# A decoder block on one Trainium2 core: expert tiles ordered by token group, two accumulators, and the final normalisation moved into the tile loop

## The reference

```
shared = (silu(x @ shared_gate.T) * (x @ shared_up.T)) @ shared_down.T
probs = sigmoid(x @ router_w.T + routing_bias)
scores, indices = top_k(probs, 2);  scores = scores / sum(scores)
w[t, indices[t]] += scores[t]                      # 8 experts, 2 per token
combined = sum_e w[:, e] * ((silu(x @ gate_w[e]) * (x @ up_w[e])) @ down_w[e])
x = layernorm(x + shared + combined)               # no gain, eps 1e-5
```

## Time and profile before

| | us |
|---|---|
| median of 3 runs (lowest, highest) | 1850.27 (1849.88, 1854.23) |
| profiled execution: time / span in the trace | 1854.46 / 1852.8 |
| TensorE busy | 1686.3 (91% of the span) |
| VectorE, ScalarE, POOL busy | 1183.4, 807.0, 720.3 |
| tile loop: first y starts / last y starts | 1147.3 / 1800.36 |
| from the last y's end to the end of the span | 52.0 |

### The profile page before, as it was taken

The page is one execution under the profiler, slowest core; times in us unless marked ns, Lnnn a source line. Parts: engine busy times, 40 slices in busy tenths (PEclk is TensorE's granted clock), DMA queues, the critical chain, the costliest instruction groups (busy, mean ns, idle before and its releaser), DMA issues.

```text
span 1852.8 us, 35774 instructions
## 1 busy us (share of the span) xinstructions
PE 1686.3 (91%) x9652; PEld 1435.5 (77%) x9653; DVE 1183.4 (64%) x2682; ACT 807.0 (44%) x1507; POOL 720.3 (39%) x625
## 2 busy tenths in 40 slices
PE   6999968999947999999999997999999999999980
PEld 5777747888845888888888875888888888888870
DVE  6888867888835676676666766555555555555546
ACT  5888766777622323223233243333333333333326
POOL 1111117888822345445344354333333333333333
PEclk9999988999977999999999998999999999999995
DMA  4555475777633222222232244333333333333329
GB/s 140 180 197 201 154 260 149 248 248 248 230 114 129 70 94 81 81 104 78 72 104 81 80 161 133 53 58 53 58 53 58 53 56 55 56 55 53 58 44 362
DMA packets 137705, 220.64 MB, mean 119 GB/s; under 512 B 40544, under 2 KB 110368, under 8 KB 129328
## 3 DMA queue, kind: packets, MB, share of 16 engines
q1 hardware_dynamic: 112064, 184.44, 30.2%
q0 software_dynamic: 25584, 35.54, 10.9%
HBM read 122.79 MB, written 97.12 MB: 119 GB/s over the span
## 4 chain that ended last, share of the span: by engine, by line
PE 38%; DMA 16%; issue 6%; DVE 4%; POOL 3%; ACT 2%; SPq 0%; POOLq 0%; ACTq 0%; another core or an unknown queue 0%; DVEq 0%
DMA acc<-back_y,back_token 14%; PE back_ps L2482 10%; PE back_ps L2384 5%; PE back_ps L2502 5%; PE back_ps L2370 4%; PE back_ps L2361 3%; PE back_ps L2280 2%; POOL back_turned_qk L1733 2%; PE back_ps L2315 2%; ACT back_out L1901 2%; PE back_ps L2323 2%; PE back_ps L2491 1%; DVE back_y L2237 1%; PE back_ps L2302 1%; PE back_ps L2268 1%
## 5 line engine op out<-in xcount | busy, mean ns | idle before, releaser
L2482 PE MATMUL back_ps<-back_w_gu,back_xe_T 128*128 x1620 | 413.0, 404 | 1.5 <-DVE back_xe_T L2218 1.5
L1764 POOL DMA_INDIRECT acc<-back_y,back_token x135 | 209.2, 1549 | 461.5 <-DVE back_y L2237 364.2
L2482 PEld LDWEIGHTS back_ps<-back_w_gu,back_xe_T 128*128 128x128 f32 x1620 | 297.4, 189 | 61.6 <-issue 2.4
L2502 PE MATMUL back_ps<-back_w_down,back_he_T 128*128 x1620 | 225.3, 288 | 1.5 <-DVE back_he_T L2230 1.5
L2502 PEld LDWEIGHTS back_ps<-back_w_down,back_he_T 128*128 128x128 f32 x1620 | 200.7, 188 | 1.8 <-issue 1.7
L1183 PE MATMUL front_ps<-front_xn_T,front_w_in_parts 128*128 128x512 f32 x768 | 187.7, 401 | 5.2 <-issue 3.3
L1721 POOL DMA_INDIRECT sorted<-back_x,back_slot x128 | 136.7, 1068 | 135.1 <-DVE back_slot L2050 100.8
L1183 PEld LDWEIGHTS front_ps<-front_xn_T,front_w_in_parts 128*128 128x128 f32 x768 | 144.3, 191 | 42.1 <-issue 6.3
L2226 DVE TENSOR_TENSOR back_h<-back_h,back_ps 128x512 f32<-128x512 f32 x135 | 92.9, 688 | 121.3 <-PE back_ps L2482 121.3
L1014 DVE SCALAR_TENSOR_TENSOR front_conv<-front_ps,front_conv_wb,front_conv 128x508 f32<-128x508 f32 (+2 forms) x192 | 140.8, 740 | 43.7 <-ACT front_conv L844 38.0
L1895 ACT ACTIVATE back_he_T<-back_ps 128x512 fp32r<-128x512 f32 x135 | 80.8, 599 | 199.9 <-PE back_ps L2491 199.9
(11 more groups left out here) (230 smaller groups left out, 3010.8 us busy)
## 6 DMA issues: line engine op xcount, KB each, us to landing
back_xe<-sorted SPq DMA_DIRECT2D x135, 136.0 KB, 2.5
gate_T<-front_gate_T SPq DMA_DIRECT2D x16, 1024.0 KB, 4.7
xc_T<-front_xc_T SPq DMA_DIRECT2D x16, 1024.0 KB, 5.6
front_xc_in<-xc_T SPq DMA_DIRECT2D x16, 1024.0 KB, 5.3
front_gate_in<-gate_T SPq DMA_DIRECT2D x16, 1024.0 KB, 6.4
front_x_rows<-in_x SPq DMA_DIRECT2D x16, 512.0 KB, 5.4
front_c_rep<-c_parts SPq DMA_DIRECT2D x128, 64.0 KB, 4.2
front_rows_in<-in_x SPq DMA_DIRECT2D x16, 512.0 KB, 7.1
```

Of the source, the lines that this page charges most:

```text
L1764: pool.indirect_dma_start(out=d["acc"][:, :], out_offset=bass.IndirectOffsetOnAxis(ap=token[:, r:r + 1], axis=0), in_=y[:, r % 2], in_offs ...
L2482: op = nc.tensor.matmul(dst[:, r % 2], xe_T[:, x_part, k], w_gu[:, bass.ds(e, 1), m, w_part, k], start=(n == 0), stop=(n == len(PASSES) - 1))
L2502: op = nc.tensor.matmul(ps_y[:, 0:D_MODEL], he_T[:, h_part, k], w_down[:, bass.ds(e, 1), w_part, k], start=(n == 0), stop=(n == len(DOWN_P ...
```

## The change

Five things change together.

1. The tiles come in the order of token groups. `run` is kept for every group, `plan_tiles` counts for each group and expert how many tiles have been opened by then, and a slot's number is the running sum over (group, expert). So the first 8 (g + 1) + 7 tiles hold all rows of groups 0 to g.
2. Tiles with an even number add to `acc`, those with an odd one to a second DRAM tensor, `more`, which SP clears group by group during the first stage. An add waits for the add two before it. Rows that don't belong to a tile are sent to 128 spare rows (`spare`) and no longer to a real token with weight zero.
3. From quad 5 on, each turn of the loop also handles half a group of 256 tokens, five quads behind: SP loads the half from `acc` and `more` (512 KB), VectorE adds them (r = 1) and takes the moments (r = 2), POOL takes the root (r = 2), VectorE makes the bias and ScalarE normalises two slices (r = 3), SP stores 256 KB in the next quad. 29 of 32 halves are handled so, and three (`end_...`) after the loop.
4. Token numbers are kept in float32, and the order of tokens within a half is changed so that a half is one piece of memory.
5. The part of SBUF for POOL's DMA descriptors is halved (`dynamic_dma_scratch_size=8192`), and the buffers for the halves lie in what is gained.

```diff
+        def in_quads(eng, body):
+            body(0, False)
+            with eng.Fori(1, BEHIND) as quad:
+                body(quad, False)
+            body(BEHIND, False, 0)
+            with eng.Fori(BEHIND + 1, QUADS - 1) as quad:
+                body(quad, False, quad - BEHIND)
+            body(QUADS - 1, True, QUADS - 1 - BEHIND)
...
                     if not (last and r >= tiles - 2):
                         rows(i + 2, (r + 2) % 4)
+                    if f is not None:
+                        half(f, r, last)
                     if not (last and r == tiles - 1):
                         up(i + 1, (r + 1) % 4)
...
+                    sp.dma_start(d["more_rows"][a], pad[:, 0:D_MODEL].unsqueeze(1).to_broadcast([P, GS, D_MODEL])
+                                 ).then_inc(more_cleared, 16)
...
             def body(quad, last, f=None):
                 for r in range(LAST - 2 if last else 4):
                     sp.wait_ge(row_ready, 2 * (4 * quad + r + 1))
                     load(4 * quad + r + 2, r % 2, 4 * quad + r + 1)
+                    if f is not None and r == 0:
+                        if not is_at(f, 0):
+                            store_half(f - 1)
+                            sp.wait_ge(half_sum_ready, f)
+                        sp.wait_ge(added[0], 16 * (2 * f + 8))
+                        sp.wait_ge(added[1], 16 * (2 * f + 7))
+                        for dst, src in ((half_in, "acc_half"), (half_more, "more_half")):
+                            sp.dma_start(dst, d[src][f]).then_inc(half_loaded, 16)
-            sp.wait_ge(added, 16 * TILES)
-            for g in range(GROUPS):
-                sp.dma_start(total[:, g], d["acc_rows"][g]).then_inc(total_loaded[g], 16)
-            for g in range(GROUPS):
-                sp.wait_ge(out_ready, GS * (g + 1))
-                sp.dma_start(d["out"][g], out[:, g]).then_inc(out_stored, 16)
+            store_half(HALVES - 4)
+            sp.wait_ge(e_up_done, TILES)
+            sp.wait_ge(added[0], 16 * 4 * GROUPS)
+            sp.wait_ge(added[1], 16 * (4 * GROUPS - 1))
+            load_end(0)
+            sp.wait_ge(added[0], 16 * ((TILES + 1) // 2))
+            sp.wait_ge(added[1], 16 * (TILES // 2))
+            load_end(1)
+            load_end(2)
...
             def add(i, r):
                 pool.wait_ge(y_ready, i + 1)
-                if not is_at(i, 0):
-                    pool.wait_ge(added, 16 * i)
+                if not early(i):
+                    pool.wait_ge(added[r % 2], 8 * (i - r % 2))
                 pool.indirect_dma_start(
-                    out=d["acc"][:, :], out_offset=bass.IndirectOffsetOnAxis(
+                    out=d[("acc", "more")[r % 2]][:, :], out_offset=bass.IndirectOffsetOnAxis(
                         ap=token[:, r:r + 1], axis=0),
-                    in_=y[:, r % 2], in_offset=None, compute_op=ALU.add).then_inc(added, 16)
+                    in_=y[:, r % 2], in_offset=None, compute_op=ALU.add).then_inc(added[r % 2], 16)
...
+            def normalise_half(f):
+                act.wait_ge(half_bias_ready, f + 1)
+                for s in range(HALF):
+                    nc.scalar.activation(half_sum[:, s], half_sum[:, s], ACT.Identity, scale=half_rstd[:, s:s + 1],
+                                         bias=half_bias[:, s:s + 1]).then_inc(half_out_ready, 1)
...
+            def half(f, r, last):
+                if r == 1:
+                    add_half(f)
+                if r == 2:
+                    half_moments(f)
+                if r == 3:
+                    half_bias_of(f)
...
-    nc = bacc.Bacc("TRN2", target_bir_lowering=False, num_devices=1)
+    nc = bacc.Bacc("TRN2", target_bir_lowering=False, num_devices=1, dynamic_dma_scratch_size=8192)
```

More of the change, by code:

```diff
@@ L1406, in decoder_back @@
         slot_f = at("slot_f", small + 2.3125, [P, 2, GS])
[L1407 to L1411, removed]
+        run = at("run", -1.75, [P, GROUPS + 1, EXPERTS])
+        count_i = at("count_i", -7.75, [P, GROUPS + 1, EXPERTS], I32)
+        tiles = at("tiles", -7.125, [P, GROUPS + 1, EXPERTS])
+        opened = at("opened", -6.5, [P, GROUPS, EXPERTS])
+        before_tile = at("before_tile", -6, [P, GROUPS, EXPERTS])
+        ends = at("ends", -5.5, [P, 3, GROUPS * EXPERTS])
+        columns = at("columns", 194.59375, [P, 2 * GS + 3])
+        spare = at("spare", -1.1875, [P, SLOT_TILES])
         neg_half = at("neg_half", 194.65625, [P, 2 * GS])
@@ L1569, in early, with no_half, in_tiles @@
             return isinstance(g, int) and g < 2
+        def in_quads(eng, body):
[6 more added lines that the diff above has]
+            body(QUADS - 1, True, QUADS - 1 - BEHIND)
         def no_tile(i, r):
             pass
-        def in_tiles(eng, turn_x, up, turn_h, down, rows=no_tile):
+        def no_half(f, r, last):
+            pass
+        def in_tiles(eng, turn_x, up, turn_h, down, rows=no_tile, half=no_half, end_tile=2):
             rows(0, 0)
@@ L1580, in in_tiles, with body @@
             turn_x(1, 1)
-            def body(quad, last):
+            def body(quad, last, f=None):
                 tiles = LAST if last else 4
@@ L1697, in _, with store_half, body @@
             store_base(GROUPS - 1)
-            def body(quad, last):
+            def store_half(f):
+                sp.wait_ge(half_out_ready, HALF * (f + 1))
+                sp.dma_start(d["out_half"][f], half_sum).then_inc(half_stored, 16)
+            def body(quad, last, f=None):
                 for r in range(LAST - 2 if last else 4):
@@ L1782, in _ @@
+            for n in range(3):
+                end_root(n)
         @block.scalar
@@ L2074, in plan_tiles @@
                 dve.wait_ge(places, PLACES * GROUPS)
-                then(nc.vector.tensor_tensor(count_i, run, plan[:, PLAN_LESS], ALU.subtract))
+                last = EXPERTS - 1
+                less = plan[:, PLAN_LESS].unsqueeze(1)
+                at_ends = ends[:, 0].rearrange("p (g e) -> p g e", g=GROUPS)
+                end_steps = ends[:, 2].rearrange("p (g e) -> p g e", g=GROUPS)
+                rows_end = run[:, GROUPS:]
+                first_rows = before_tile.rearrange("p g e -> p (g e)")
@@ L2076, in plan_tiles @@
+                then(nc.vector.tensor_tensor(count_i, run, less.to_broadcast([P, GROUPS + 1, EXPERTS]), ALU.subtract))
                 then(nc.vector.tensor_scalar(count_i, count_i, 7, None, ALU.arith_shift_right))
                 then(nc.vector.tensor_copy(tiles, count_i))
-                then(nc.vector.tensor_tensor_scan(ends[:, 0], plan[:, PLAN_ONES], tiles, 0.0, ALU.mult, ALU.add))
-                then(nc.vector.tensor_scalar(ends[:, 1], tiles, -float(P), float(REGION), ALU.mult, ALU.add))
@@ L2080, in plan_tiles @@
-                then(nc.vector.tensor_tensor(ends[:, 2, 0:EXPERTS - 1], run[:, 1:], run[:, 0:EXPERTS - 1], ALU.subtract))
-                then(nc.vector.memset(ends[:, 2, EXPERTS - 1:], -1e6))
+                then(nc.vector.tensor_tensor(opened, tiles[:, 1:], tiles[:, 0:GROUPS], ALU.subtract))
+                then(nc.vector.tensor_tensor_scan(ends[:, 0], plan[:, PLAN_ONES], opened.rearrange("p g e -> p (g e)"), 0.0,
+                                                  ALU.mult, ALU.add))
+                then(nc.vector.tensor_tensor(before_tile, tiles[:, 1:], at_ends, ALU.subtract))
@@ L2259, in _ @@
+            in_tiles(dve, turn_x, up, turn_h, down, rows, half)
+            half_bias_of(HALVES - 4)
+            end_moments(0)
+            end_bias_of(0)
+            for n in (1, 2):
+                end_moments(n)
+            for n in (1, 2):
+                end_bias_of(n)
         @block.tensor
@@ L2450, in add_ends @@
                 pe.wait_ge(planned, PLANNED + COEF)
-                for q, of in enumerate((None, 1, 2)):
-                    lhs = plan[0:EXPERTS, PLAN_UNIT] if of is None else coef[:, of]
-                    op = nc.tensor.matmul(ps_plan[:, q], lhs, past, start=True, stop=True)
+                changes = slice(0, P - 1)
+                nc.tensor.matmul(ps_plan[0:1, 0], columns[changes, 2 * GS + 2:], past[changes], start=True, stop=True)
+                for q in (1, 2):
+                    op = nc.tensor.matmul(ps_plan[:, q], coef[changes, q], past[changes], start=True, stop=True)
                 op.then_inc(ends_turned, 1)
@@ L2554 @@
            "delta": [TOKENS], "x1": [GROUPS, P, GS, D_MODEL],
-           "sorted": [SORTED, ROW], "acc": [TOKENS + P, D_MODEL]}
+           "sorted": [SORTED, ROW], "acc": [TOKENS + P, D_MODEL],
+           "more": [TOKENS + P, D_MODEL]}
 def program(nc, t):
```

228 lines of the change are left out of this document (155 added, 73 removed).

## The result

| | before | after |
|---|---|---|
| median of 19 runs each (lowest, highest), us | 1852.67 (1849.65, 1854.23) | 1854.64 (1849.87, 1859.35) |
| profiled execution: time / span | 1854.46 / 1852.8 | 1853.05 / 1851.1 |

The ratio of after to before is 1.0014, 95% interval 1.0008 to 1.0021: 2.6 us slower, well inside the 0.3% that count as no change. The forecast was 15 us faster, with a range up to 1847; the time lies outside it.

What follows compares the result with a forecast made beforehand. TensorE was taken to pace the 135 tiles, with a 52.0 us tail where it does nothing. Terms -33.1 + 16.8 + 1.0 + 0.3 = -15.0 us took 1850.3 to 1835.3 us; range 1816 to 1847.

Steps and rivals of the forecast that it cites:

- What bounds the kernel: Tile loop: TensorE paces the 135 tiles, 4.885 us each; the add chain costs nothing until the end.
- The rival in which the adds set the pace: Tile loop: adds pace the tiles, so two accumulators quicken the loop by 13 us, to 1822; chance 3%.
- The tail, -33.1: After the last y: 52.0 us shrinks to 18.9 with only three halves left, saving 33.1 us.
- The loop, +16.8: Tile loop: normalisations ahead of the silu make TensorE start 0.6 us late at r = 3, 28 times.
- slack of 0.42 us: Tile loop: h could end 0.42 us later before delaying TensorE's transposes, so r = 2 loses nothing.
- 1.0 each (28 us) if the statistics at r = 2 overrun too: Tile loop: upper bound of the loss per half; as a rival, slips near 1 us each give 1846, chance 8%.
- The start, +1.3: Before the tiles: 1.0 us for the longer plan and 0.3 for clears and an extra register instruction a group.
- my 1.0 for what reaches the first y: Plan of the tiles: 2.1 us more VectorE work, of which 1.0 delays the first tile; bounds 0 and 2.1.
- the clears I took 0.3: Before the tiles: sixteen 512 KB clears of `more` in SP's queue, with register instructions, cost 0.3 us; bounds 0 and 3.
- the halved descriptor space I took 0: POOL's scatters: halving the descriptor store costs nothing; the other bound was 2 us or more for each of 128 scatters.
- transfers of the halves holding up tiles: Tile loop: loads in SP's queue land 0.9 us late in each quad, giving 1860 us; chance 8%.
- the root holding h: Tile loop, r = 2: POOL's root holds VectorE's h, 0.9 us more a half, 26 in all, 1861 us; chance 2%.

Runs made afterwards that it cites:

- e7: The kernel before with only the space for POOL's DMA descriptors halved (8192); ratio to before 1.0017.
- e4: The changed kernel with the half's normalisations behind the silu and TensorE's owner load ahead of the wait for h; 1828.59 us.
- e1: The changed kernel with the half's two normalisations moved behind the transposes' copies of the same tile; 1831.65 us.
- e12: The kernel before with four useless 640-wide ScalarE copies ahead of the silu of each quad's first tile, and halved descriptor space; ratio 1.0156.
- e2: The changed kernel with TensorE's owner load moved ahead of the wait for h, normalisations still ahead of the silu; 1831.2 us.

## Why the prediction was wrong, step by step

- **What bounds the kernel:** right. TensorE paces the tiles, 20 tiles without halves take as long with two accumulators (97.63 and 97.71), and the adds have left the chain. The rival in which the adds set the pace is out.
- **The tail, -33.1:** right, -34.0. The add, landing, load and the work of two halves came in the order written; the loads came 1.5 us later and the store landed 2.3 us sooner than written, so the number is closer than its terms.
- **The loop, +16.8, is the step that failed.** The chain bias, two normalisations, silu, h was right: h should end 0.95 us late, and was 0.81 late, 0.14 of it from r = 2. Wrong was the slack of 0.42 us between the end of h and TensorE, which I read from when the transposes of h start. The sum counted only what is late beyond that slack, 0.6 a quad. The wait in TensorE's queue also holds back the register load behind it, which must be done before the next gate matmuls, and for those there is no slack. Hence 0.14 was lost at r = 2, where I had written that nothing is lost, and 0.67 at r = 3, and with the 0.2 that stay open it is 1.0 a quad, 28.3 in all, for a forecast of 0.6. The bound of "1.0 each (28 us) if the statistics at r = 2 overrun too" was the case that came, with its own time of 1846, and I gave it 8%. That 1846 is 9 us below the measured median comes from the start, 2.8 us more than its sum, and from the median of before, 1850.3 over three runs and 1852.7 over nineteen; the rest is the spread of single executions told of below. Had I written down everything that TensorE issues behind the wait, which I did for VectorE's and ScalarE's queues, that case would have been the forecast.
- **The start, +1.3:** +4.1 in the profiled execution. The plan's own work took 1.7 more, of the 2.1 that I had for it. Whether my 1.0 for what reaches the first y is right stays open: from the plan's start to the first y it is 37.5 us before and 37.4 after, so nothing, but 35.7 in e7, which has the plan of before, so 1.6. For the clears I took 0.3 and they cost 0.7 to 4.1; for the halved descriptor space I took 0 and it cost 1.3 to 5.0. The reason for the 0, that nothing in the trace waits for a descriptor's place, was a misreading: the scatter at 1100.82, late by "issue" in the kernel before, moved with the size of the space. How the clears cost time stays open; no single row shows it.
- **The rivals:** transfers of the halves holding up tiles (no such wait; e4 is at full pace) and the root holding h (the root's rows lie beside VectorE's at their usual lengths) are out. The sum with the measured terms, 4.1 + 0.1 + 28.3 - 0.1 - 34.0 = -1.6, gives the spans' difference. The ratio of all runs says +2.6 with 1.5 to 3.9: the profiled execution of before lies 1.8 above its median and that of after 1.6 below. Much of that can arise early: after and the five kernels e1 to e4, alike up to the plan, reach it anywhere from 1113.99 to 1116.28.

## What to carry to other kernels

Slack of an operation is not the gap to the next instruction that waits for it, but the least over everything behind that wait in its queue, register loads included, down to the work that must follow without a gap. Where a queue must block on another engine, load what the next work needs (indices, registers) ahead of the wait: here one moved load gave h 0.5 us of slack and took back 24 us. And work for an engine with idle time belongs behind the critical operation of that engine, not ahead of it.

## What the runs showed of the hardware

- A register load on TensorE's queue has no busy time in the profile. Where the queue had just been held at a wait, the matmuls behind it came 0.55 us (e12) to 0.78 us (after) later than the 0.43 us of e2, which has the load ahead of the wait.
- Two ScalarE operations of one column took 0.66 us together, those of 256 columns 1.09: so the width makes up less than half of the 1.09.
- Four ScalarE copies of 128x512 one behind the other took 2.18 us, 0.545 each, where a single 128x512 operation between waits took 0.60 (that one reads PSUM and writes float32, the copies read SBUF and write bf16).
- With the space for POOL's descriptors halved, POOL's scatters stalled at the 57th and 105th, 1.2 to 1.4 us each, in all eleven such kernels; with the full space the 114th stalled by 1.8 us, in the three others.
